# The first attention layer of a four-layer graph network: the third relation's scores by way of W q, and its projection behind the pair's

## The reference, cut to what matters

```python
x = _layernorm(x + L0(x))   # two RGCN convolutions, each with a query gate
x = _layernorm(x + L1(x))   # one GCN convolution
x = _layernorm(x + L2(x))   # two relational attention convolutions
x = _layernorm(x + L3(x))   # two GCN convolutions
```

```python
def rgat_conv(x, W, q, k, b, src, dst, etype, heads, out_ch, n_nodes):
    xr = jnp.einsum('nd,rdf->rnf', x, W)
    oi = xr[etype, dst]
    oj = xr[etype, src]
    qi = oi @ q
    kj = oj @ k
    alpha = jax.nn.leaky_relu(qi + kj, NEG_SLOPE)
    m = jax.ops.segment_max(alpha, dst, num_segments=n_nodes)
    e = jnp.exp(alpha - m[dst])
    z = jax.ops.segment_sum(e, dst, num_segments=n_nodes)
    a = e / (z[dst] + EPS)
    msg = (a[:, :, None] * oj.reshape(-1, heads, out_ch)).reshape(-1, heads * out_ch)
    out = jax.ops.segment_sum(msg, dst, num_segments=n_nodes)
    return out + b
h = jax.nn.elu(rgat_conv(x, W1, q1, k1, b1, src, dst, edge_type, 4, 192, n))
out = rgat_conv(h, W2, q2, k2, b2, src, dst, edge_type, 1, 768, n)
```

## Time and profile before

| what | value |
|---|---|
| median of 3 runs | 266.5 us (266.43 to 267.36) |
| the profiled execution, its own time | 266.77 us |
| its span, first to last instruction | 264.7 us |
| outside the span | 2.07 us |
| TensorE busy / VectorE / ScalarE / GpSimd | 247.8 / 155.2 / 89.1 / 84.2 us |
| mean granted TensorE clock | 0.996 |
| chain that ended last, by engine | PE 65%, POOL 10%, DVE 9%, ACT 6%, issue 5%, DMA 4% |
| gates' products on the chain | POOL L621 |
| the first attention layer, from the turned nodes to the weighted sums | 200.31 to 220.99 us |

### The profile page before, as it was taken

How to read it: one execution, slowest core, us unless ns; L and a number is a source line. 1 busy time by engine, 2 the same in 40 slices (tenths; PEclk the granted TensorE clock), 3 DMA queues, 4 the chain that set the end, 5 groups by cost and what they waited for, 6 DMA issues and landing times.

```text
span 264.7 us, 4922 instructions
## 1 busy us (share of the span) xinstructions
PE 247.8 (94%) x2037; PEld 127.2 (48%) x2037; DVE 155.2 (59%) x280; ACT 89.1 (34%) x151; POOL 84.2 (32%) x78
## 2 busy tenths in 40 slices
PE   8899999997999999899999998899998988999994
PEld 4675654443545542367765222225563443445572
DVE  0845322617887999841027999995667367405322
ACT  2323210008676995320003576770302013013000
POOL 7581000006997799300001778770000000000000
PEclk9999999999999999999999999999999999999998
DMA  7999999899802969200999910005999545000001
GB/s 237 373 401 399 401 315 154 140 354 404 313 1 45 402 268 355 9 0 15 271 408 401 402 58 2 0 2 142 395 403 402 208 143 217 0 0 2 0 2 30
DMA packets 39911, 53.46 MB, mean 202 GB/s; under 512 B 22985, under 2 KB 23753, under 8 KB 39890
## 3 DMA queue, kind: packets, MB, share of 16 engines
q1 hardware_dynamic: 29792, 51.64, 54.9%
q10 hardware_dynamic: 10098, 1.52, 3.5%
HBM read 52.17 MB, written 0.20 MB: 198 GB/s over the span
## 4 chain that ended last, share of the span: by engine, by line
PE 65%; POOL 10%; DVE 9%; ACT 6%; issue 5%; DMA 4%; SPq 1%; DVEq 0%; POOLq 0%
PE ps L1142 12%; PE ps L1258 11%; PE ps L1110 10%; POOL prod L621 6%; POOL W L621 4%; PE ps L1157 4%; DMA W<-in_L_gnn_Wg 4%; PE ps L1536 3%; PE ps L1347 3%; PE ps L1616 3%; PE ps L1227 3%; PE ps L1086 3%; ACT pre L702 2%; PE ps L1404 2%; DVE prod L912 2%
## 5 line engine op out<-in xcount | busy, mean ns | idle before, releaser
L621 POOL TENSOR_TENSOR prod<-pre,qn 128x768 f32<-128x768 f32 x28 | 54.3, 1955 | 12.5 <-ACT pre L702 12.5
L920 DVE TENSOR_TENSOR pre<-ps,qg 128x768 f32<-128x768 f32 x46 | 43.1, 950 | 6.3 <-PE ps L1404 3.4
L702 ACT ACTIVATE pre<-pre 128x768 f32<-128x768 f32 x46 | 38.5, 848 | 5.5 <-DVE pre L920 5.0
L1258 PE MATMUL ps<-W 128*128 128x384 f32 x96 | 35.2, 492 | 0.7 <-ACT W L458 0.4
L458 ACT COPY W<-ps 128x384 f32<-128x384 f32 x35 | 16.0, 482 | 24.9 <-PE ps L1086 24.7
L702 ACT ACTIVATE ps<-ps 128x768 f32<-128x768 f32 x18 | 14.2, 794 | 29.6 <-PE ps L1333 21.4
L1347 PE MATMUL ps<-prod,rsel 128*32 128x384 f32 x192 | 20.5, 497 | 1.8 <-POOL prod L621 1.0
L1258 PEld LDWEIGHTS ps<-W 128*128 128x128 f32 x96 | 17.1, 190 | 10.3 <-issue 2.2
L1142 PE MATMUL ps<-W,prod 128*64 128x256 f32 (+1 forms) x240 | 20.6, 328 | 0.0
L1142 PEld LDWEIGHTS ps<-W,prod 128*64 128x64 f32 x240 | 15.1, 137 | 4.9 <-issue 0.5
L1086 PE MATMUL ps<-ident,W 128*128 128x128 f32 x108 | 16.7, 282 | 0.8 <-DMA W<-in_L_gnn_Wg 0.4
(11 more groups left out here) (244 smaller groups left out, 336.6 us busy)
## 6 DMA issues: line engine op xcount, KB each, us to landing
W<-in_L_gnn_W SPq DMA_DIRECT2D x9, 2304.0 KB, 12.8
W<-in_L_gnn_W_rel SPq DMA_DIRECT2D x6, 2304.0 KB, 17.3
W<-in_L_gnn_W_root SPq DMA_DIRECT2D x2, 2304.0 KB, 16.4
W<-in_L_gnn_Wq SPq DMA_DIRECT2D x4, 1152.0 KB, 9.4
qn<-in_L_gnn_query_embs SPq DMA_DIRECT2D x4, 384.0 KB, 10.0
W<-in_L_gnn_Wg SPq DMA_DIRECT2D x3, 384.0 KB, 3.9
W<-in_L_gnn_Wg SPq DMA_DIRECT2D x1, 1152.0 KB, 9.5
W<-in_L_gnn_Wg SPq DMA_DIRECT2D x12, 96.0 KB, 4.0
```

What stands on the lines that cost most here:

```text
L621: nc.gpsimd.tensor_tensor(prod_of(T), pre_of(T), qn[:, pair_and_node(t)[0], :], ALU.mult).then_inc(prod_p, 1)
L702: nc.scalar.activation(tile, tile, ACT.Sigmoid).then_inc(sig_ready, 1)
L920: nc.vector.tensor_tensor(dst, ring(T), by_half(qg[:, pair_and_node(T % TILES)[0], :]), ALU.add).then_inc(pre_ready, 1)
L1258: ins = nc.tensor.matmul(ps[:, unit_bank(u), 0:HD], qT[:, k, p * P:(p + 1) * P], WgT_q[:, k, c * HD:(c + 1) * HD], start=(k == 0), stop=(k ...
```

## The change

- `L2_W1_2`, relation 2's weight of the first attention layer, is fetched a second time, in 24 block transfers by SyncE, into slot 4 (`L2_W1T`), at the place where `L2_W2_0` was fetched. The first copy stays in slot 6.
- VectorE turns it: six block transposes, `turn_w1`, dealt out 2, 3, 1. The first two stand behind the second gate's tanh, the next three where three `v_units` stood, the last behind the turned nodes.
- TensorE forms `VT1` = (W q)^T and (W k)^T (`w1_scores`, 12 calls with 32 stationary columns and 384 moving ones): eight calls in place of the five `keep_warm` of the second layer norm, four inside the pair. ScalarE copies it out, six small matmuls turn it and add two partial sums (`V1`), ScalarE copies `V1` out, and six products of `V1` with `nodeT` give relation 2's score inputs. The six transposes of `X2`, VectorE's copy of them (L1000) and the six products with q and k go.
- The pair's 12 rounds come first. Relation 2's six rounds come behind them: one ahead of `turn_pair(1)`, one behind it, one behind the last `times_qk`, three behind the scores. The `keep_warm` between, one and four, go.
- The copies of `X2` out of PSUM stand behind the softmax on VectorE and ScalarE, and the weighted sums wait for them.
- `V_AT` is 2, 1, 3, 4, 2; `L2_W2_0` goes to slot 0 after `alpha_done`, `L2_W2_1` to slot 4 after `VT1` is summed, behind `L3_W1`. In the second attention layer the six products with `V` stand four rounds later.

```diff
-            ("L2_W2_0", 4, 1), ("L2_W2_1", 0, 1), ("L2_W2_2", 1, 1), ("L3_W1", 5, 1), ("L3_W2", 2, 1)]
+            ("L2_W1T", 4, 6), ("L2_W2_0", 0, 1), ("L2_W2_1", 4, 1), ("L2_W2_2", 1, 1), ("L3_W1", 5, 1), ("L3_W2", 2, 1)]
...
+        VT1 = prod[:, 2, 0:HD]
+        V1_f = prod[:, 2, HD:HD + KC * GN]
+        V1 = V1_f.rearrange("p (k c) -> p k c", k=KC)
+        VT_BANK, V1_BANKS = 5, (3, 4)
...
-        V_AT = (3, 3, 4, len(V_UNITS) - 10)
+        V_AT = (2, 1, 3, 4, 2)
+        W1T_AT = (2, 3, 1)
...
             sp.wait_ge(reduced, TILES)
             for c, name in enumerate(("q", "k")):
                 sp.dma_start(qk_rows[c], a[f"L2_gnn_{name}2"].rearrange("f o -> o f").to_broadcast([P, D])).then_inc(qk_rows_loaded, 16)
             load("L2_W1_1", a["L2_gnn_W1"][1])
-            load("L2_W2_1", a["L2_gnn_W2"][1], alpha_done, 4)
+            load("L2_W2_0", a["L2_gnn_W2"][0], alpha_done, 4)
             load("L2_W2_2", a["L2_gnn_W2"][2])
             load("L3_W1", a["L3_gnn_W1"], proj_done, 2)
-            load("L3_W2", a["L3_gnn_W2"], rel_done, 3)
+            load("L2_W2_1", a["L2_gnn_W2"][1], VT1_done, 1)
+            load("L3_W2", a["L3_gnn_W2"], rel_done, 2)
             sp.wait_ge(x_ready, 11)
             sp.dma_start(out[:, 0:HD], t0[0:N, :]).then_inc(out_stored, 16)
...
-            act.wait_ge(rel_done, 1)
-            nc.scalar.copy(X2[:, HD:D], ps[N:P, 2, 0:HD]).then_inc(X_out_s, 1)
-            act.wait_ge(rel_done, 3)
+            act.wait_ge(VT1_done, 1)
+            nc.scalar.copy(VT1, ps[:, VT_BANK, 0:HD]).then_inc(VT1_ready, 1)
+            act.wait_ge(V1_done, 1)
+            nc.scalar.copy(V1_f.rearrange("p (c f) -> p c f", c=2),
+                           ps[:, V1_BANKS[0]:V1_BANKS[1] + 1, 0:JC * GN]).then_inc(V1_ready, 1)
+            act.wait_ge(rel_done, 2)
             nc.scalar.copy(X01[:, HD:D], ps[:, 1, 0:HD]).then_inc(X_out_s, 1)
...
+            act.wait_ge(rel_done, 3)
+            nc.scalar.copy(X2[:, HD:D], ps[N:P, 2, 0:HD]).then_inc(X_out_s, 1)
...
+            def turn_w1(stage):
+
+                at = sum(W1T_AT[:stage])
+                for k in range(at, at + W1T_AT[stage]):
+                    dve.wait_ge(loaded["L2_W1T"][k], 16 * (P // GN))
+                    nc.vector.transpose(W1T[:, k, :], W1T[:, k, :]).then_inc(W1T_ready, 1)
+
...
                     link(nc.vector.tensor_tensor(hh[:, :], hh[:, :], xa[:, :], ALU.add))
+                    turn_w1(0)
                 for i, cols in enumerate(PARTS_OF):
...
-            v_units(0)
+            turn_w1(1)
...
+                turn_w1(2)
+                v_units(0)
+                dve.wait_ge(rel_done, 1)
+                nc.vector.tensor_copy(X01[:, 0:HD], ps[:, 0, 0:HD]).then_inc(X_out_v, 1)
                 v_units(1)
-                dve.wait_ge(rel_done, 3 * layer + 1)
-                nc.vector.tensor_copy(X2[:, 0:HD], ps[0:N, 2, 0:HD]).then_inc(X_out_v, 1)
-                dve.wait_ge(X_turned, 3 * layer + 1)
-                nc.vector.tensor_copy(XT[:, :, P:n], ps[:, 5, 0:HD].rearrange("p (k n) -> p k n", k=KC)).then_inc(XT_out_v, 1)
-                dve.wait_ge(rel_done, 3 * layer + 2)
-                nc.vector.tensor_copy(X01[:, 0:HD], ps[:, 0, 0:HD]).then_inc(X_out_v, 1)
-                dve.wait_ge(X_turned, 3 * layer + 2)
+                dve.wait_ge(X_turned, 1)
                 nc.vector.tensor_copy(XT[:, 0:JC, 0:P], ps[:, 3, 0:HD].rearrange("p (k n) -> p k n", k=JC)).then_inc(XT_out_v, 1)
                 v_units(2)
...
+                dve.wait_ge(rel_done, 3)
+                nc.vector.tensor_copy(X2[:, 0:HD], ps[0:N, 2, 0:HD]).then_inc(X_out_v, 1)
...
+            dve.wait_ge(X_turned, 3)
             nc.vector.tensor_copy(XT[:, 0:JC, 0:P], ps[:, 3, 0:HD].rearrange("p (k n) -> p k n", k=JC)).then_inc(XT_out_v, 1)
+            v_units(4)
             dve.wait_ge(qk_done, 2)
...
+            def w1_scores(ks):
+
+                for k in ks:
+                    if k == 0:
+                        pe.wait_ge(qk_loaded, 64)
+                    pe.wait_ge(W1T_ready, k + 1)
+                    for c in range(2):
+                        at = c * N + k % 2 * GN
+                        ins = nc.tensor.matmul(ps[at:at + GN, VT_BANK, 0:HD], qk[:, k, 0, :], W1T[:, k, c * HD:(c + 1) * HD],
+                                               start=(k < 2), stop=(k >= KC - 2), skip_group_check=True)
+                return ins
...
-                if n > 1:
+                if n == 2:
+                    w1_scores(range(0, 4))
+                elif n > 1:
...
+                project_pair(0, BY_BLOCK[:4], as_copied(nodeT_ready, 4))
+                w1_scores(range(4, KC)).then_inc(VT1_done, 1)
+                project_pair(0, BY_BLOCK[4:]).then_inc(rel_done, 1)
+                pe.wait_ge(VT1_ready, 1)
+                for c in range(2):
+                    for j in range(JC):
+                        ins = nc.tensor.matmul(ps[:, V1_BANKS[c], j * GN:(j + 1) * GN], VT1[c * N:(c + 1) * N, j * P:(j + 1) * P],
+                                               qsel[c * N:(c + 1) * N, :], start=True, stop=True, skip_group_check=True)
+                ins.then_inc(V1_done, 1)
+                project_pair(1, BY_BLOCK[:2])
+                pe.wait_ge(V1_ready, 1)
+                turn_pair(0)
+                project_pair(1, BY_BLOCK[2:4])
+                for k in range(KC):
+                    g, h, j = k % (P // GN), k // JC, k % JC
+                    nc.tensor.matmul(ps[g * GN:(g + 1) * GN, ACC, OTHER], V1[:, k, :], nodeT[:, j, h * N:(h + 1) * N],
+                                     start=(k == g), stop=(k + P // GN >= KC), skip_group_check=True)
+                pe.wait_ge(XT_out_v, 1)
+                times_qk(range(JC))
+                project_pair(1, BY_BLOCK[4:]).then_inc(rel_done, 1)
...
+                wait_loaded(pe, keys[2])
+                alone = dict(T=nodeT, w=W[SLOT[keys[2]]], bank=2)
...
                     nc.tensor.matmul(ps[:, SCORE[h], 0:n], ident_b[:, :], maskb[:, :], start=True, stop=False,
                                      skip_group_check=True)
-                keep_warm(1, 5)
+                project(chunks=BY_BLOCK[:1], last=False, **alone)
                 turn_pair(1)
-                pe.wait_ge(XT_out_s, layer + 1)
...
+                project(chunks=BY_BLOCK[1:2], first=False, last=False, **alone)
+                pe.wait_ge(XT_out_s, 1)
+                times_qk(range(JC, KC)).then_inc(qk_done, 1)
+                project(chunks=BY_BLOCK[2:3], first=False, last=False, **alone)
...
+                project(chunks=BY_BLOCK[3:], first=False, **alone).then_inc(rel_done, 1)
                 ins = add_bias(f"L2_gnn_b{layer + 1}", ADDEND)
                 ins.then_inc(addend_done, 1)
-                keep_warm(4, ACC)
...
+                        if b == 0:
+                            pe.wait_ge(X_out_v, 2)
+                            pe.wait_ge(X_out_s, 2)
...
-            pe.wait_ge(v_sum, len(V_UNITS))
-            for k in range(KC):
-                g, h, j = k % (P // GN), k // JC, k % JC
-                nc.tensor.matmul(ps[g * GN:(g + 1) * GN, ACC, SINGLE2], V[:, k, :], nodeT[:, j, h * N:(h + 1) * N],
-                                 start=(k == g), stop=(k + P // GN >= KC), skip_group_check=True)
-            pe.wait_ge(XT_out_v, 3)
+            pe.wait_ge(XT_out_v, 2)
...
+            pe.wait_ge(v_sum, len(V_UNITS))
+            for k in range(KC):
+                g, h, j = k % (P // GN), k // JC, k % JC
+                nc.tensor.matmul(ps[g * GN:(g + 1) * GN, ACC, SINGLE2], V[:, k, :], nodeT[:, j, h * N:(h + 1) * N],
+                                 start=(k == JC), stop=(k + P // GN >= KC), skip_group_check=True)
```

79 lines of the change are left out of this document (34 added, 45 removed).

## The result

| | before | after |
|---|---|---|
| median of 20 runs, us | 266.52 (266.25 to 267.36) | 265.56 (265.38 to 266.62) |
| ratio, 95% interval | | 0.9967 [0.9961, 0.9973] |
| profiled execution: time, span, us | 266.77, 264.7 | 265.61, 263.9 |

The change gains 0.33%, where 1.4 us (0.53%) were forecast: the time lies inside the range and 0.5 us above its centre, and by the 0.5% named in the prediction the outcome is "the same", which had a chance of 0.45 there against 0.47 for "faster". The interval still excludes no change.

The account below looks back on a forecast made before the run. Bound: a TensorE-led chain whose waits relation 2's rounds could fill. Stretch 3.73 + 0.2 - 0.78 - 0.80 - 0.47 = 1.9 us; 1.83 after ScalarE's copies, less 0.40 for the norm: 1.4 off, median 265.1, range 264.3 to 266.5.

Parts of the forecast that it names:

- (a): Four `w1_scores` added inside the pair on TensorE: taken at 0.78 us, with ends 0.68 and 0.85.
- (b): Turning of `VT1` on TensorE, 6 calls, 12 instructions: taken at 0.80 us, between 0.43 and 1.02.
- second norm: Eight `w1_scores` for five `keep_warm` delay the mean's matmul: norm ends 0.40 us later (0.27 to 0.61).
- signs of being right: Mean 1.5 us behind GCN projection; turning 0.8; no TensorE wait over 0.1 from pair to sums; sums 18.9 after pair's start.
- signs of being wrong: Waits for `L2_W1T`, `L2_W1_1` or `L2_W2_0`; GpSimd products over 1.9 us; TensorE waiting for second-attention copy; turning over 1.02.
- the other two groups with that credit: Second transposes and last products on TensorE; with the bias, each to lap over the next row by 0.07, 0.2 together.
- Waits and rows that go: On TensorE between pair and weighted sums: `X2` transposes, `keep_warm`, waits and a gap between transposes go, 3.73 us in sum.
- The lone rounds: Rounds standing alone on TensorE cost more: one 0.80, three at the end 1.93; 18 rounds take 0.47 us more.
- the thinnest: Cover of VectorE's copy in the second attention layer: ends about 230.7, wanted 230.81; each 0.1 us late is lost.
- The third rival: Softmax still ends last, uncovered by three closing rounds; 265.9 if one unit held VectorE; disturbed gate or late softmax: 0.23.
- The first and second rivals: First: block fetch slows GpSimd's second-gate products, 266.1 to 266.5 (0.23 with late softmax); second: slow SyncE issue, 276.6 (0.08).
- The slower case: SyncE issues 24 blocks at over 1.9 us each, so `L2_W1_1` lands late: far above 267.8, chance 0.08.

## Why the prediction came out as it did

**The mechanism was right, and the gain in the sum too high by 0.5 us.** By the steps of the prediction:

| step | forecast | measured in the changed kernel |
|---|---|---|
| four scores in the pair, (a) | 0.78 | 204.11 - 203.32 = 0.79 |
| turning, (b) | 0.80 (0.43 to 1.02) | 206.58 - 205.55 = 1.03 |
| mask, bias | 0.18, 0.2 | 212.22 - 211.95 = 0.27, 218.88 - 218.62 = 0.26 |
| transposes to sums, ScalarE's copies | 0.94 | 219.93 - 218.88 = 1.05 |
| pair's start to sums | 18.85 | 19.34 |
| second norm | +0.40 (0.27 to 0.61) | +0.44 |
| gain, norm taken off | 1.4 | 0.90 in the trace, 0.96 between medians |

**By its own signs it did worse than by its time.** Of the four signs of being right one came, the mean at 1.43 us for 1.5. The turning took 1.03 and not 0.8, a wait of 0.17 is left where none over 0.1 was to be, and the sums start after 19.34 us and not 18.9. Of the signs of being wrong one came, if barely: the turning over 1.02. Its likeliest outcome by a hair was "faster"; it came out "the same".

**The step that was mis-sized most is (b).** It stood in the sum with 0.80 us and measured 1.03. I had two rows, a dear one with the same stationary shape and a cheap one with the narrow moving operand, and took a value between them. The cheap row, the products, has a stationary operand of 32 columns where the turning loads 128. The dear row's 1.02 would have been right, but by luck. It is made of transposes on one half of the rows, 0.061 us a step, and I took a transpose for the price of a matmul instruction; the turning is two series of matmul instructions at 0.112 us that overlap in part. The two errors cancel. Where the rule of the Trainium skill (TensorEngine Tiling (Array Packing), Instruction Overhead) and my mixture differed, the rule's 1.02 was right for the sum; but its reason, that short matmuls cost a fixed time, isn't what the runs show, since the same twelve took 0.79 in another order.

**Smaller misses.** The mask costs 0.27 in front of a float32 round and 0.17 in front of `keep_warm`; I had carried it unchanged. The bias was credited with lapping over the next row by 0.07 and did not (0.27 before, 0.26 now); the other two groups with that credit did. That a change of type or shape is dearer than a repeat is argued, not shown. ScalarE's copies came 0.1 later, as its copy of `X2` starts only at 218.84, when the last round has ended; the experiment that moved it shows that nothing is gained by the other order.

**What was right.** Waits and rows that go: all, apart from the 0.17 left at the sums. The lone rounds: 213.02 - 212.22 = 0.80, and 218.62 - 216.69 = 1.93 for the three at the end. The norm: eight scores in front of the mean, shown by splitting them; but +0.40 against +0.44 is luck in part, since the part ahead of the mean was 0.34 and the 0.10 behind it was not in the sum. The work at no cost: the fetch, the block transposes, the units, each under cover as named; the thinnest was where I put it, with 0.24 us left where 0.1 was forecast. The third rival, softmax last, fails: TensorE has no wait at 218.88. The first and second rivals fall with the experiment without the fetch and with the rows of GpSimd and SyncE. The slower case needed 1.9 us per issue and met 0.93.

## What to carry over

Work that is free to stand anywhere is worth the holes it fills, no more: price the new way alone (here, with the norm that it held up, it was dearer than the old one by 1.5 us) and count the holes apart. Whatever is put ahead of a short matmul that others wait for, a layer norm's mean above all, delays them by all that it reaches past the moment when the inputs are ready (here four scores cost nothing and eight 0.62 us); behind it, in the norm's own wait, the same work is free. To price a short matmul, look for a row of the same kind of instruction with the same stationary columns, and ask on which rows of the array the calls stand: a transpose is no price for a matmul, and calls on two halves overlap.

## What the hardware showed unexpectedly

- Twelve float32 matmul instructions (six calls) with 64 stationary rows, 128 stationary and 32 moving columns took 1.03 us with three calls on one half of the rows and then three on the other, and 0.79 with the halves by turns. In both orders they stand 0.112 us apart in two series; only the start of the second moves, from 0.25 us behind the first to 0.006.
- A float32 transpose of 64 x 128 is one instruction, 0.06 us from the next on its half of the rows, where a float32 matmul of the same stationary shape is two of 0.112. Six took 0.33 us on two halves and 0.51 on one.
- Behind three `keep_warm` or behind the scores the mean's matmul of a norm cost 0.10 us more than behind five; its first weight load began with it and not 0.21 us ahead.
- 24 transfers of 96 KB in pieces of 128 bytes, issued by SyncE in 22.3 us beside the gate, slowed no engine by an amount that a row shows.
